# Moving three pieces of softmax and normalisation work between engines in an attention and MLP block

## What is computed

```python
def _layer(x, wqkv, qs, ksc, wo, lg, lb, w1, b1, w2, b2):
    h = shift_token(x)                    # second half of the columns taken from the token before
    q, k, v = split(h @ wqkv, 3)          # 8 heads of 64
    q = l2norm(q) * qs; k = l2norm(k) * ksc
    q, k = rotary_xpos(q, k)
    o = local_attention(q, k, v)          # window 128: own tile of 128 keys and the one before
    x = x + o @ wo
    h = shift_token(x)
    h = (h - mu) / sqrt(var + 1e-05) * lg + lb
    h = h @ w1 + b1
    a, g = split(h, 2)
    return x + (a * gelu(g)) @ w2 + b2
...
x = x + 0.5 * _L0_ffn_ref(_layernorm(x), ...)     # two layers
x = x + _L0_attn_ref(_layernorm(x), ...)          # the scan, "mid" in the kernel
x = x + 0.5 * _L0_ffn_ref(_layernorm(x), ...)     # two layers
```

## Time and profile before

| | us |
|---|---|
| median of 3 runs | 2616.13 (2615.41 to 2616.23) |
| the profiled execution, its own time | 2615.41 |
| its span in the profile | 2613.6 |

### The profile page before, as it was taken

How to read it: one execution, slowest core, us unless ns; L and a number is a source line. 1 busy time by engine, 2 the same in 40 slices (tenths; PEclk the granted TensorE clock), 3 DMA queues, 4 the chain that set the end, 5 groups by cost and what they waited for, 6 DMA issues and landing times. The chain is left out here.

```text
span 2613.6 us, 79938 instructions
## 1 busy us (share of the span) xinstructions
PE 2494.9 (95%) x29664; PEld 2229.8 (85%) x29664; DVE 1975.4 (76%) x6501; ACT 1808.1 (69%) x5192; POOL 1579.0 (60%) x1799
## 2 busy tenths in 40 slices
PE   8899999999999999999999999999999999999999
PEld 7788888888888888888767888888888888888888
DVE  7877788777777777776656777777777788877776
ACT  5777777776777777676454777767667777767765
POOL 5666666666666666664213566666666666666665
PEclk9999999999999999999999999999999999999999
DMA  3122011012000000004101000000003100000000
GB/s 122 34 83 78 27 42 54 22 54 85 14 2 2 2 11 17 2 30 176 35 18 34 2 3 2 2 2 2 2 2 119 34 3 18 18 18 18 18 18 26
DMA packets 75955, 82.19 MB, mean 31 GB/s; under 512 B 37552, under 2 KB 61872, under 8 KB 74416
## 3 DMA queue, kind: packets, MB, share of 16 engines
q1 hardware_dynamic: 74272, 75.61, 8.9%
q10 hardware_dynamic: 1296, 1.46, 0.2%
HBM read 49.53 MB, written 26.74 MB: 29 GB/s over the span
## 5 line engine op out<-in xcount | busy, mean ns | idle before, releaser
L634 POOL TENSOR_TENSOR pr<-pr,rden 128x384 f32<-128x384 f32 (+1 forms) x480 | 409.7, 871 | 363.3 <-DVE rden L1751 362.9
L834 ACT ACTIVATE pr<-pr,nb 128x192 f32<-128x192 f32 (+1 forms) x1024 | 437.9, 429 | 150.1 <-DVE nb L1742 150.1
L1134 PE MATMUL bank<-h2T,w 128*128 128x256 f32 x1408 | 405.7, 288 | 38.6 <-DVE h2T L1784 38.6
L1135 PE MATMUL bank<-h2T,w 128*128 128x256 f32 x1408 | 395.7, 281 | 0.0
L1136 PE MATMUL bank<-h2T,w 128*128 128x256 f32 x1408 | 395.6, 281 | 0.0
L1742 DVE CUSTOM_DVE_ANT_0 pr<-bank,maskb,r 128x192 f32<-128x192 f32 (+1 forms) x1024 | 347.8, 397 | 16.6 <-PE bank L1197 9.8
L676 POOL TENSOR_TENSOR uTl<-t,uTh 128x256 fp32r<-128x256 f32 x288 | 214.4, 749 | 239.7 <-ACT uTh L934 238.9
L1846 DVE SCALAR_TENSOR_TENSOR t<-bank,b,t 128x256 f32<-128x256 f32 (+1 forms) x384 | 181.8, 480 | 173.6 <-ACT t L919 91.3
L1134 PEld LDWEIGHTS bank<-h2T,w 128*128 128x128 f32 x1408 | 267.3, 190 | 46.1 <-DVE h2T L1784 45.1
L1134 PE MATMUL bank<-wqkv,hT 128*128 128x512 f32 x768 | 304.6, 397 | 1.4 <-DVE nb L1742 1.3
L1135 PE MATMUL bank<-wqkv,hT 128*128 128x512 f32 x768 | 302.5, 394 | 0.0
(11 more groups left out here) (245 smaller groups left out, 7073.5 us busy)
## 6 DMA issues: line engine op xcount, KB each, us to landing
wqkv<-wqkv_split SPq DMA_DIRECT2D x18, 512.0 KB, 6.7
w<-w_split SPq DMA_DIRECT2D x3, 2816.0 KB, 9.9
Y<-in_x SPq DMA_DIRECT2D x8, 512.0 KB, 7.5
stt<-stt SPq DMA_DIRECT2D x256, 3.0 KB
out<-Y SPq DMA_DIRECT2D x8, 512.0 KB, 3.9
h<-out SPq DMA_DIRECT2D x7, 512.0 KB, 4.0
out<-h SPq DMA_DIRECT2D x7, 512.0 KB, 3.0
stt<-stt SPq DMA_DIRECT2D x192, 0.0 KB
```

Of the source, the lines that this page charges most:

```text
L634: e.tensor_tensor(probs(j, t), probs(j, t), rden[:, 2 * j:2 * j + 2].unsqueeze(2).to_broadcast([P, 2, w]), ALU.mult).then_inc(pn_done, 1 i ...
L834: last = e.activation(probs(j, t)[:, g, :], probs(j, t)[:, g, :], ACT.Exp, bias=nb[:, hd:hd + 1], scale=-1.0, accum_out=den[:, hd:hd + 1])
L1134: e.matmul(out, left[0], right[0], start=first, stop=False)
L1135: e.matmul(out, left[0], right[1], start=False, stop=False)
```

## The change

Four things are moved, and nothing is added or left out.

1. In tile 0, piece 2 of the probabilities is normalised by VectorE (`NP_first(L, b, 2)`) and no longer by GpSimd; `squares` of k moves ahead of it. `XB` of tile 0 moves on GpSimd from behind piece 1 to behind the power for q.
2. In tiles 1 to 3, VectorE makes the rotary products of the next k behind the reciprocal `R(1)` (before: behind `R(2)`) and their sum behind `R(2)` (before: behind `R(3)`).
3. In the MLP part, VectorE makes `LN_moments` of part 2 behind `U(1)` (before: in front of it) and `LN_apply` of part 2 behind `U(2)` (before: in front of it).
4. For tile 3, the DMA of `move_first_halves` is issued by ScalarE, behind the table load for Gelu and in front of the first `G`, and no longer by SyncE.

```diff
@@ SyncE: move_stats
                 e.dma_start(stt[1:P, t, 6:12], stt[0:P - 1, t + 1, 18:24]).then_inc(q, 16)
-                move_first_halves(e, t, q)
+                if t < 3:
+                    move_first_halves(e, t, q)
                 if t:
                     e.dma_start(stt[P - 1:P, t, 12:18], stt[0:1, t, 0:6]).then_inc(q, 16)
@@ GpSimd: NP
-                                ALU.mult).then_inc(pn_done, 1 if t or j < 2 else 2)
+                                ALU.mult).then_inc(pn_done, 1 if t or j == 0 else 3)
@@ GpSimd: sequence
-                    for j in range(4 if t else 3):
-                        if prev and t == 0 and j == 2:
-                            XB(*prev, t)
+                    for j in range(4 if t else 2):
                         NP(L, b, t, j)
                     if ahead:
                         A1_k(*ahead)
@@
                     if ahead:
                         A1_q(*ahead)
+                    if prev and t == 0:
+                        XB(*prev, t)
@@ ScalarE: sequence
                 table(ACT.Gelu)
+                e.wait_ge(st_done, at(st_done, idx(L, b, 3) + 1))
+                move_first_halves(e, 3, st_moved[1])
                 for mt in range(MT):
                     G(L, b, 0, mt)
@@ TensorE: PT
-                if t or j < 3:
+                if t or j < 2:
                     e.wait_ge(pn_done, at(pn_done, 4 * n + j + 1))
                 else:
-                    e.wait_ge(pn_first, at(pn_first, 8 * L + b + 1))
+                    e.wait_ge(pn_first, at(pn_first, 2 * (8 * L + b) + j - 1))
@@ VectorE: sequence, tile 0
                         R(L, b, t, 1)
                         rotary(*ahead, 0)
+                        squares(idx(*ahead), 0)
                         R(L, b, t, 2)
-                        squares(idx(*ahead), 0)
+                        NP_first(L, b, 2)
                         if L == 0 and b == 0:
                             entry_apply(0, 2)
                         R(L, b, t, 3)
@@ VectorE: sequence, tiles 1 to 3
                             R(L, b, t, j)
+                            if ahead and j == 1:
+                                rotary(*ahead, 0)
                             if ahead and j == 2:
-                                rotary(*ahead, 0)
+                                rotated(*ahead, 0)
                         if ahead:
-                            rotated(*ahead, 0)
                             squares(idx(*ahead), 0)
                         WO(L, b, t - 1)
@@ VectorE: sequence, MLP part
                     U(L, b, 0, mt)
                     if mt == 0:
                         LN_apply(L, b, 1)
+                    if mt == 1:
                         LN_moments(L, b, 2)
-                    if mt == 1:
                         U_rest(L, b, 0)
+                    if mt == 2:
                         LN_apply(L, b, 2)
```

## The result

The changed kernel takes **2647.56 us** (median of 4 runs, 2646.5 to 2649.02) against 2615.85 us for the kernel before on the same chip (2615.41 to 2616.23): the ratio is 1.0121, with a 95% interval of 1.0104 to 1.0139. It is 31.7 us slower. The forecast was 2633 us, slower, with a range of 2590 to 2652. The profiled execution took 2651.15 us, 35.7 us more than the profiled one before, and its span is 2649.3 us.

What follows compares the result with a forecast made beforehand. TensorE, busy 95% of the span, was taken as the bound. Terms of -48 (MLP part), +25 (tile 0), +35 (tiles 1 to 3) and +5 (tile 3) gave +17 us on 2615.41, so 2633 us, range 2590 to 2652.

Steps and rivals of the forecast that it cites:

- The likeliest case: Whole kernel: slower, 2621 to 2650 us, given a chance of 0.59.
- the one term of the MLP part: MLP part: job 6's wait for `h2T` and most of the transposes' wait go, 1.5 us x 32 = -48 us.
- The attention part: Tiles 0 to 3: losses of +25 us in tile 0, +35 us in tiles 1 to 3, +5 us more in tile 3.
- the sign of being wrong: MLP part: job 6 still waiting over 0.3 us for `h2T` would show the forecast wrong there.
- Tile 0: Tile 0: k's wait goes, but late `XB` makes `WO` 0.8 us later (0.28 to 1.01), +25 us over 31 rounds.
- The case I gave 0.2 to 0.4 us to: Tile 0: guard starts 0.02 us ahead of the normalisation, so scaling blocks the sum of q by only 0.2 to 0.4 us.
- Tiles 1 to 3: Tiles 1 to 3: piece 2 meets the sum of k, delaying piece 3; 0.36 us x 96 = +35 us, tile 3 +5 us.
- piece 3's row: Tiles 1 to 3, profile before: piece 3 on GpSimd started 0.12 us behind the sum of k and took 1.26, not 0.8 us.
- the rival in which it gets the port: Tiles 1 to 3: piece 2 starts before the sum of k, costing nothing there; faster, 2577 to 2593 us, chance 0.19.
- the 0.3 that the prediction looked for: Tiles 1 to 3: sign that transposes of the probabilities (L1217) wait about 0.3 us for GpSimd in 96 tiles.
- No change: Rival: sum of q not blocked in tile 0 and MLP part gives 1.55 us; 2611 to 2621 us, chance 0.17.
- The power holds the port: Rival, tile 0: sum of k waits behind the power, q 1.6 us and `WO` 1.9 us later; 2667 us, chance 0.05.

Runs made afterwards that it cites:

- both runs of it alone: Kernel before with only the MLP part's reordered norm work: 2595.82 us with one DMA issued by ScalarE too, 2595.7 us with all three on SyncE.
- edit 3 alone: Kernel before with only `LN_moments` behind `U(1)` and `LN_apply` behind `U(2)` in the MLP part, all DMAs on SyncE: 2595.7 us, ratio 0.993.
- edits 1 and 2 alone: Two runs against the kernel before: only tile 0's moves, 2650.54 us (+35.6); only the earlier rotary products and sum in tiles 1 to 3, 2645.9 us (+30.9).

## Why the prediction was right, and where it was not

**The bound** held: TensorE, at 96%. The wait for k went, and that of job 6 all but went. The likeliest case came, slower; the sum was 14.6 us too low. That the time fell inside the range is partly luck: the one term of the MLP part was forecast 33.6 us too good, and with it alone put right the sum would be 2667 us, outside. The attention part was forecast some 14 us too dear, and that took part of it back.

**The MLP part is the term that was mis-sized:** -1.5 us a round forecast (bounds -1.2 and -1.55), -0.45 measured, and -0.45 in both runs of it alone (medians of 14 steady rounds). Four steps of the estimate failed. (1) "The last one left on SyncE is issued one place earlier" is true, its issue starts 1.89 instead of 2.80 us behind job 0, but the statistics don't start earlier for it (4.64 and 4.65 us). (2) `h` was to end at 1127.3 to 1127.9 in the round of the earlier trace rows; on that scale it ended at 1120.36 + 8.08 = 1128.44. I carried the 1.26 us of the earlier trace rows over, although GpSimd's work beside it had changed. (3) `h2T` was to be ready at 1129.6 at the latest; job 6 got it at 1077.34, which is 1130.37 on that scale, and still lost 0.28 us, just under the 0.3 that the prediction named as the sign of being wrong. (4) I took the transposes' wait as going too (0.15 us); it grew from 6.5 us in 26 places to 22.4 in 59, since each `h` now ends later than TensorE wants it. `U_rest` beside the power is shown as one cause by the run that moved it (7.0 us against edit 3 alone). That `U_lo` stretches `h` is read from the traces alone (1.26 us with one beside it, 1.62 or 1.63 with two in three kernels); no run took them away.

**Tile 0:** +0.8 us forecast (0.28 to 1.01), +0.60 measured with `WO`. The steps held: `XB` is last, `W2` waits for it, `oT` and `WO` behind it. The case I gave 0.2 to 0.4 us to, the guard first and a short block of the sum of q, is the one that came (0.19). The text missed that piece 3 has no slack of its own: VectorE's two normalisations make the transposes of the probabilities 0.5 us longer. Here it costs nothing, since `WO` waits for `XB` anyway; with `XB` in place it is the price of the edit, and why the k transposes start 0.7 and not 1.2 us earlier. It also missed the after-effect in tile 1, which the runs put at `XB` (0.62 us with `XB` alone moved) and which edit 2 happens to absorb; had the 0.63 and 0.39 us of tile 1 in edits 1 and 2 alone added up there, some 20 us more would have been lost. That too was luck.

**Tiles 1 to 3:** 0.36 us in each and 0.15 more in tile 3 forecast, 1.23 us a round together. Measured 0.29, 0.33 and 0.39, 1.01 together. Piece 2 was blocked (1.24 us), as piece 3's row said; the rival in which it gets the port is out. The matmuls' list shows 0.17 us a tile for it, under the 0.3 that the prediction looked for; start to start it is the 0.33 of the table. In tile 3 the sum of q did meet the scaling (1.42 us at 1061.72), for 0.06 us at TensorE.

**The sum:** a round was to cost 0.8 + 1.23 - 1.5 = 0.53 us and cost 1.16; of the 0.63 between them the MLP part is 1.05, and the attention part was forecast 0.42 too dear.

**The rivals.** "No change" would have needed the MLP part's 1.55 us. "The power holds the port" is out: the sum of k ran its 0.69 us from 1018.18 while the power ran from 1017.58 to 1019.25. The Trainium skill (SBUF — State Buffer, Who interferes with whom) says that the one that issues first holds the shared ports for the whole instruction; for the scaling and the sum of q the trace agrees again (in tile 3 the scaling started 0.17 us ahead, and the sum took 1.42 us), for the power on 128x8 it doesn't, and the measurement decides. The same section lists `tensor_scalar` among the instructions that can take the shared pair; that fits `h` at 1.62 us beside `U_lo`, though no run here tells that apart from other causes.

## What to carry to other kernels

Moving work off an engine that is ahead of the bound pays nothing by itself: ask for each moved instruction what is queued behind it and which consumer lost its slack, above all for the small one that is put last (`XB`, 0.73 us long, decided 30 us). A duration from the trace holds only for the company that it had there: when an order changes, look what now runs beside it on the engine that it can collide with. Price a wait by what follows it, from start to start of the bound engine's groups, and look at its weight loads too; and don't add the costs of edits that lie on one chain.

## What the runs showed of the hardware that was not expected

- A small DMA inside SBUF isn't seen earlier when its issue moves up. Before, the third of three issues of SyncE started at 1123.16 us and the statistics at 1125.01, 1.85 us later; after, with the second one on ScalarE's queue, 1069.22 and 1071.97, 2.75 us. From the first issue it is 3.43 and 3.44 us. These are SyncE's issues after:

```profile
1068.53 0.65 SPq L405 DMA_DIRECT2D stt<-stt  x1
1069.22 1.28 SPq L409 DMA_DIRECT2D stt<-stt  x1
```

  This last issue took 0.82 us before, and takes 1.26 to 1.36 us in 27 of 32 rounds. In 4 it still took 0.84, and there the statistics started no earlier (845.18 to 847.95, 2.77 us), so the longer issue isn't what delays them. The statistics wait for all three DMAs together, and the profile doesn't tell which lands last; it may be the one issued first, whose place didn't change. That is open.
- A GpSimd instruction of eight columns beside VectorE's sum can be stretched (the guard 0.24 to 0.68 us) or leave it untouched (the power, and the sum's 0.69 us), by which came first and which instruction it is. So with the power of three columns and `U_rest`: 0.85 us with `U_rest` 0.37 us behind its start, 1.08 with `U_rest` 0.05 us ahead, and `U_rest` takes 0.42 us both times.
- The costs of edits on one chain were far from additive: 35.6 + 30.9 - 19.2 = 47.3 us for the parts, 31.7 for the whole.
